# Layer 0's depthwise stage: results stored from the scalar engine's queue instead of the sync engine's

## The reference

```
base = _conv1x1(x, w_qkv)                       # 192 -> 576 channels
qkv = jnp.concatenate([_dwconv(base, w_dw3, 1), _dwconv(base, w_dw5, 2), _dwconv(base, w_dw7, 3)], axis=1)
qkv = _conv1x1(qkv, w_pconv)                    # 1728 -> 576 channels
```

## Time and profile before

| what | value |
|---|---|
| time, median of 3 runs | 2519.12 us (2515.17 to 2522.4) |
| profiled execution, its own time | 2517.25 us |
| its span in the trace | 2515.5 us |
| depthwise stage, first batch's end to last batch's end | 99.6 to 557.3 us |
| TensorE busy over the span | 1945.1 us (77%) |
| ScalarE busy over the span | 804.7 us (32%) |
| SyncE's queue, share of 16 DMA engines over the span | 58.8% |
| ScalarE's queue, the same | 1.1% |

### The profile page before, as it was taken

How to read it: one execution, slowest core, us unless ns; L and a number is a source line. 1 busy time by engine, 2 the same in 40 slices (tenths; PEclk the granted TensorE clock), 3 DMA queues, 4 the chain that set the end, 5 groups by cost and what they waited for, 6 DMA issues and landing times. The chain is left out here.

```text
span 2515.5 us, 36893 instructions
## 1 busy us (share of the span) xinstructions
PE 1945.1 (77%) x15660; PEld 1203.3 (48%) x15660; DVE 1287.4 (51%) x1313; ACT 804.7 (32%) x1269; POOL 870.2 (35%) x459
## 2 busy tenths in 40 slices
PE   3879779769999999999978768777777777774052
PEld 1577666667777777777734322222222222221031
DVE  6445444441111111111271166799999999988803
ACT  3445445440000000000122125633543533335410
POOL 3334233220000000000000040599899899983300
PEclk9889899889999999999988778899899979987555
DMA  7899999988131313130120040678688868863799
GB/s 197 249 311 314 316 292 304 296 257 241 59 118 59 118 60 118 60 118 1 43 59 11 0 139 21 156 197 219 171 213 216 209 175 213 218 179 90 224 215 294
DMA packets 195538, 424.51 MB, mean 169 GB/s; under 512 B 18733, under 2 KB 143661, under 8 KB 184717
## 3 DMA queue, kind: packets, MB, share of 16 engines
q1 hardware_dynamic: 182540, 414.81, 58.8%
q10 hardware_dynamic: 12832, 7.34, 1.1%
HBM read 299.33 MB, written 121.96 MB: 167 GB/s over the span
## 5 line engine op out<-in xcount | busy, mean ns | idle before, releaser
L743 PE MATMUL ps<-mem 128*128 128x288 f16 x5376 | 654.6, 287 | 14.4 <-DMA mem<-depthwise_out 14.4
L743 PEld LDWEIGHTS ps<-mem 128*128 128x128 f16 x5376 | 502.1, 98 | 152.9 <-issue 15.4
L1717 POOL TENSOR_TENSOR mem<-mem 128x1024 f32<-128x1024 f32 x192 | 465.7, 2444 | 45.3 <-ACT mem L1651 42.9
L1626 PE MATMUL ps<-mem 128*128 128x512 f32 x768 | 417.9, 676 | 39.1 <-POOL mem L1717 35.0
L1112 POOL TENSOR_TENSOR mem<-mem 128x1536 f16<-128x1536 f32 x16 | 50.8, 3180 | 940.3 <-ACT mem L1090 940.3
L533 PE MATMUL ps<-mem 56*96 56x240 f16 (+1 forms) x5184 | 308.2, 280 | 86.1 <-DMA mem<-base_phases 53.0
L533 PEld LDWEIGHTS ps<-mem 56*96 56x96 f16 x5184 | 297.7, 128 | 111.4 <-DMA mem<-base_phases 58.5
L786 DVE TENSOR_TENSOR mem<-ps,mem 128x128 f16<-128x128 f32 x64 | 18.7, 292 | 586.8 <-ACT mem L807 586.8
L1746 DVE TENSOR_TENSOR_SCAN mem<-mem,ps 128x1024 f32<-128x1024 f32 x132 | 307.8, 2332 | 18.2 <-issue 10.3
L646 DVE TENSOR_TENSOR mem<-ps,mem 96x1024 f16<-96x1024 f32 x144 | 175.3, 1220 | 217.9 <-ACT mem L578 217.9
L1626 PEld LDWEIGHTS ps<-mem 128*128 128x128 f32 x768 | 153.5, 213 | 242.9 <-issue 134.5
(11 more groups left out here) (202 smaller groups left out, 1915.4 us busy)
## 6 DMA issues: line engine op xcount, KB each, us to landing
mem<-l_bc SPq DMA_DIRECT2D x504, 256.0 KB, 4.5
depthwise_out<-mem SPq DMA_DIRECT2D x105, 512.0 KB, 9.4
mem<-depthwise_out SPq DMA_DIRECT2D x31, 1664.0 KB, 10.8
mem<-base_phases SPq DMA_DIRECT2D x72, 448.0 KB
base_phases<-mem SPq DMA_DIRECT2D x56, 512.0 KB, 9.9
mem<-in_wd SPq DMA_DIRECT2D x72, 336.0 KB
mem<-l_planes SPq DMA_DIRECT2D x48, 252.0 KB
mem<-in_x SPq DMA_DIRECT2D x4, 2048.0 KB, 13.6
```

The source lines that it names most:

```text
L743: ins = nc.tensor.matmul(ps[:, 2 * (i % 2) + h, 0:HALF], d, pw[rows, wa, k, HALF * h:HALF * h + HALF], start=(k == 0 and n == 0), stop=(k ...
L1626: ins = nc.tensor.matmul(py[:, a, :], ident, hh[:, n % 4, 512 * a:512 * a + 512], start=(n % N == 0), stop=(n % N == N - 1))
L1717: nc.gpsimd.tensor_tensor(hh[:, n % 4, :], hh[:, n % 4, :], cs[:, n % 4, :], ALU.mult).then_inc(hc_pool, 1)
```

## The change

`store_out` moves from SyncE's list to ScalarE's. There it stands in batch n behind the copy of unit 0 and stores batch n-1. Its wait (now ScalarE's) and its three transfers are the same. Loads, base stores and the last batch's small stores stay where they were.

```diff
@@ sync engine
-            def store_out(n):
-                sp.wait_ge(dw_lo, UPB * (n + 1))
-                for k in range(3):
-                    sp.dma_start(d_dram[:, QKV * k + 2 * BP * n:QKV * k + 2 * BP * (n + 1)], stg[n % NSTG][PHASES * k:PHASES * (k + 1)]
-                                 ).then_inc(d_stored[n % NSTG], 16)
...
             for n in range(NBATCH):
-                if n >= 1:
-                    store_out(n - 1)
                 if n + 2 < NBATCH:
@@ scalar engine
+            def store_out(n):
+                act.wait_ge(dw_lo, UPB * (n + 1))
+                for k in range(3):
+                    act.dma_start(d_dram[:, QKV * k + 2 * BP * n:QKV * k + 2 * BP * (n + 1)], stg[n % NSTG][PHASES * k:PHASES * (k + 1)]
+                                  ).then_inc(d_stored[n % NSTG], 16)
...
                     unit(n, k)
+                    if k == 0 and n >= 1:
+                        store_out(n - 1)
                     if k == 1 and n + 1 < NBATCH:
                         taps(n + 1)
```

## The result

| | before | changed |
|---|---|---|
| median of 7 runs each, us | 2522.40 (2515.17 to 2527.65) | 2533.92 (2528.04 to 2537.57) |
| ratio, with its 95% interval | | 1.0044 (1.0029 to 1.0058) |
| profiled execution, us | 2517.25 | 2535.9 |

The changed kernel is slower by about 11 us.

What follows compares the result with a forecast made beforehand. The prediction took DMA transfers to bound the depthwise stage. Profiled 2517.25 us less 21 (two queues) less 1 (stage's end) gave 2495; the profile lay 1.9 under the median, so 2497 us, range 2474 to 2532.

Steps and rivals of the forecast that it cites:

- D: ScalarE's issue time for three stores per batch: 2 to 4 us, cost 0, free up to about 5.3 us.
- ScalarE held up: Rival: a full store queue stalls ScalarE in base batches, deciding from D above 5.3 us; 2537 us, chance 0.14.
- A store's issue on ScalarE takes below 1.3 us on average: Sign that the forecast is right: average issue time of one moved store on ScalarE below 1.3 us.
- Two queues side by side: Depthwise stage: loads beside stores go faster; 21 us saved, 15 in batches without base steps, 6 with.
- SyncE gets free: Windows and taps issued some 4 us earlier on SyncE; worth nothing, since DMA engines are busy.
- The stage's end: SyncE's 24 small stores, issued in 13.00 us, no longer wait behind batch 34's big stores; 1 us saved.
- The rate stays: Rival: the same busy DMA engines move the same bytes, so no change; 2518 us, chance 0.25.
- Interleaving costs: Rival: stores and loads interleaved take longer, 1.0 us more in each of 33 batches; 2550 us, chance 0.07.
- Wrong altogether would be a change outside the depthwise stage: Sign against the whole forecast: any change outside the depthwise stage, which was costed at nothing.
- The signs named ahead: Stretches without base steps fall from about 52 to 48 us, base batches keep 13.5, second queue carries about 55 MB more.

Runs made afterwards that it cites:

- e2: Kernel before, stores still on SyncE, with six idle copies on ScalarE where the change begins its stores; 2539.07 us, ratio 1.0069.
- e10: Changed kernel with stores on ScalarE only in batches without base steps, back on SyncE in the others; 2538.39 us, ratio 1.0081.
- e3: Kernel before with ScalarE's taps of the next batch put ahead of unit 0's copy, stores still on SyncE; 2511.78 us, ratio 0.9965.
- e4: Changed kernel with ScalarE's taps of the next batch put ahead of unit 0's copy; 2495.28 us, ratio 0.9897.
- e6: Changed kernel with next batch's taps ahead of unit 0's copy and base batches' stores back on SyncE; 2506.94 us, ratio 0.9938.
- e8: Changed kernel with next batch's taps ahead of unit 0's copy and ScalarE's stores behind unit 2; 2522.05 us, ratio 0.9999.
- e1: Changed kernel with ScalarE's three stores moved from behind unit 0 to behind unit 2; 2538.41 us, ratio 1.0053.

## Why the prediction was wrong

The forecast was 2497 us, in a range of 2474 to 2532, with 0.21 for slower; it is 2534, slower, 37 us above the forecast.

**The step that failed** is the cost of D in the batches without base steps: "In the batches without base steps ScalarE was busy 22.0 of 51.2 us, which leaves 7.3 us for each. I take D as 2 to 4 us and its cost as 0." The 22.0 is right and the inference is not. An engine's free share says how much work it could add, not where it may stand. For the base batches the prediction followed ScalarE's order row by row and found 2.95 us of slack; for the others it took an average. Had it followed the order there, already named the wait (GpSimd's L623, nine times, longest 2.8), and that its releaser hangs on the copy of unit 1 stands in the order of ScalarE. The cost of D, put at 0: 17 us in e2 with no transfer moved (1.0 us in a loop at full clock, more loops at the lower clock, and two splits that slid beside L668), and 20 us in e10, with the stores. The rival "ScalarE held up" had the sign but the wrong place (base batches) and the wrong point from which it decides (above 5.3 us; here under 3 was enough).

**D itself** was right: 2 to 4 us forecast for three issues, with these issue times in the changed kernel (ns, min/median/max), and three in 2.7 to 3.5 us in the rows above; only the longest lie above, 4.79 us from 244.92 at most. "A store's issue on ScalarE takes below 1.3 us on average" held.

```profile
L575 ACTq DMA_DIRECT2D depthwise_out<-mem x105: 308/642/2934, 101.4 to 565.0; - x105
```

**Two queues side by side**, minus 21 us: the mechanism was right and the size near. With the loop gone the second queue is worth 16.5 us (e3 to e4). Where it comes from was not as foretold: 15 of the 21 us were put to batches without base steps and 6 to those with, and e6 gives about 7 and 10, of which the 7 is not clear of the noise (0.9951 to 0.9979 against 0.9918 to 0.9959). In the changed kernel the gain is there as a shorter wait for windows (43.1 to 19.0), but TensorE then waits for the taps. The Trainium skill (DMA: Bandwidth & Descriptors, Rules for kernel authors) says that spreading over issuing engines doesn't help bandwidth, since all run on the same 16 engines; the share of 0.99 and 1.00 in the windows of e3 and e4 agrees with the reason, and their 320 and 335 GB/s and the 16.5 us between the kernels speak against the rule for loads beside stores. By the rule e4 would have been e3, 2512.

**SyncE gets free**, 0: no run isolates it, and e3 to e4 contains it.

**The stage's end**, minus 1 us: wrong in sign. The 24 small stores took 15.57 us instead of 13.00, though the big stores of batch 34 were in the other queue. The excess over 11.1 us was thus not a wait behind them in SyncE's own queue; what it was stays open. Nor does any run show the full queue of the rival "ScalarE held up": the three issues took 4.79 us at most.

**The rivals.** "The rate stays": no, by e4. "Interleaving costs": not for loads beside stores, but yes for result stores beside base stores, which the prediction had not looked for (it compared loads with loads in the earlier trace rows). In the changed kernel stores behind unit 0 seem to avoid most of it; behind unit 2 it costs 27 us (e4 to e8). "Wrong altogether would be a change outside the depthwise stage": there was none to speak of, 16.7 of 18.5 us of the two spans' difference stand ahead of the next stage's first matmul.

**The signs named ahead** read rightly: base batches kept 13.5 us; the second queue carried 55.1 MB more; the stretches without base steps did not get shorter, which ruled the forecast out on first sight.

## What to carry to other kernels

Before work is moved onto an engine with time to spare, follow that engine's list from the new place to whoever waits last, in each kind of iteration apart: a delay inside a loop from batch to batch costs all that exceeds the wait it replaces (1.0 of 1.94 us in e2), however idle the engine is, and putting the independent work first (here the taps) can turn the loss into a gain. In these runs stores in a queue apart from the loads were worth having where both directions were in flight, and not beside another stream of stores with small packets. When one wait gets shorter and another longer, a second limit may be hiding a gain: look for that limit before undoing the change.

## What the runs showed of the hardware that was not expected

- What stands in the second queue matters: result stores in it beside loads gained 16.5 us (e3 to e4), result stores in it beside stores of 1 KB rows made 256 GB/s, where each alone made 372 and 389, and placing them so cost 27 us (e4 to e8); that the one follows from the other is argued.
- SyncE's issues can take longer when the large stores are in ScalarE's queue, though the median doesn't (0.62 us before, 0.57 in the changed kernel): the longest issue of a shifted base store (L440) was 3.0 us before and 9.3 in the changed kernel, though the large result stores had left its queue, and the 24 small stores took 15.6 us for 13.0.
- TensorE's clock sets the period of a loop through other engines: with nothing added to it, it closed in 10.5 us where units 0 and 1 were done at a granted clock of 1.00, in 12.2 where the clock was 0.67 in the first 3.9 us (before), and in 13.6 with TensorE busy for 10.84 us instead of 7.74 (e1). The wait doesn't show it: it reads 2.8 us behind a batch of 10.5 us and behind one of 13.6, since the lower clock fell on units 0 and 1, ahead of the copies, taps and split that the wait is for; the period and the busy time show it. What decides which of them a batch gets stays open.
- VectorE's subtraction with both operands in SBUF (4.34 us) stretched GpSimd's split beside it from 1.92 to 6.74 us, by 4.8. The Trainium skill (SBUF — State Buffer, SBUF: two separate sides) states that a VectorE operation with two SBUF inputs and a GpSimd operation that reads SBUF exclude one another, the one that starts first holding the port for its whole instruction. The rows agree in the size, 4.8 us more beside 4.34; they don't show that the first comer wins, since the GpSimd subtraction that was stretched is recorded from 541.08, ahead of VectorE's at 541.69.
